# Macaron block (FFN, attention, FFN) on one core: the filler products of TensorE in the lead removed

## The reference

```python
x = x + 0.5 * ffn(layernorm(x))      # D = 128, H = 512, exact GELU
x = x + attn(layernorm(x))           # 16 heads of 64
x = x + 0.5 * ffn(layernorm(x))      # the same weights

# ffn: m1, m2 are outer products of 16 of the batch's own tokens
h   = gelu(x @ W1.T + scale * (x @ m1.T) + b1)
out = h @ W2.T + scale * (h @ m2.T) + b2
# attn: q, k with RMS norm per head; softplus gate on k; causal
bias   = -max(i - j, 0) * softplus(omega) * slope * gate[j]
scores = q @ k.T / 8 + bias
y      = softmax(scores) @ v ;  return y @ Wproj
```

## Time and profile before

| | |
|---|---|
| median of 3 runs | 755.38 us |
| the profiled execution | 754.96 us |
| its span, first to last instruction | 753.2 us |
| TensorE matmul busy | 729.2 us, 97% |
| VectorE, ScalarE, GpSimd busy | 655.4, 643.3, 645.4 us (87, 85, 86%) |

### The profile page before, as it was taken

One profiled execution on the slowest core, in us unless ns is written; L12 is line 12 of the kernel. 1 busy time (PEld: TensorE's weight loads), 2 busy tenths in 40 slices (PEclk: granted clock), 3 DMA queues, 4 the chain that ended last, 5 costly groups with the idle time before them and its releaser, 6 DMA issues.

```text
span 753.2 us, 25090 instructions
## 1 busy us (share of the span) xinstructions
PE 729.2 (97%) x9279; PEld 523.1 (69%) x9279; DVE 655.4 (87%) x2128; ACT 643.3 (85%) x1428; POOL 645.4 (86%) x760
## 2 busy tenths in 40 slices
PE   6789999999999999999999999999999999999997
PEld 4347667677768766787667777577776776677775
DVE  7889789988888798987989879888889879899986
ACT  8878798888988799888998889987998879986764
POOL 6738889898998999989998999989899898996791
DMA  6233315251345406333253423454043431435231
GB/s 176 41 93 80 73 36 138 58 113 33 73 99 100 101 3 125 77 87 87 44 104 63 102 64 72 87 102 103 14 104 84 100 87 26 105 73 113 61 58 29
DMA packets 98561, 60.05 MB, mean 80 GB/s; under 512 B 73566, under 2 KB 85344, under 8 KB 98440
## 3 DMA queue, kind: packets, MB, share of 16 engines
q1 hardware_dynamic: 98280, 57.93, 35.3%
q10 hardware_dynamic: 160, 0.52, 0.3%
HBM read 4.74 MB, written 2.10 MB: 9 GB/s over the span
## 4 chain that ended last, share of the span: by engine, by line
PE 63%; ACT 17%; DVE 12%; issue 5%; POOL 3%; DMA 0%; POOLq 0%; ACTq 0%; DVEq 0%
PE ps L1147 11%; PE ps L1149 10%; PE ps L1148 10%; PE ps L1294 8%; PE ps L1320 7%; PE ps L1321 7%; PE ps L1276 4%; ACT qk L1077 4%; DVE masked L1720 3%; PE ps L1322 3%; DVE ss L1684 2%; ACT pt L1102 2%; ACT qkn L1016 2%; ACT sq L1015 2%; ACT hid L1003 2%
## 5 line engine op out<-in xcount | busy, mean ns | idle before, releaser
L859 POOL TENSOR_TENSOR pt_l<-pt 128x512 f16<-128x512 f32 x366 | 320.2, 904 | 38.5 <-ACT pt L1102 38.2
L1720 DVE CUSTOM_DVE_ANT_0 masked<-ps,causal_row 128x512 f16<-128x512 f32 x480 | 205.8, 486 | 27.5 <-PE ps L1294 26.5
L1102 ACT ACTIVATE pt<-ps 128x512 f32<-128x512 f32 (+1 forms) x384 | 175.1, 534 | 16.6 <-PE ps L1322 16.4
L1320 PE MATMUL ps<-qk 128*128 128x512 f16 (+3 forms) x512 | 146.6, 299 | 0.1
L1321 PE MATMUL ps<-qk 128*128 128x512 f16 (+3 forms) x512 | 146.5, 299 | 0.0
L885 POOL TENSOR_TENSOR qkn<-qkn,rs 128x512 f32<-128x512 f32 x128 | 131.0, 1052 | 13.4 <-ACT rs L1027 12.8
L1147 PE MATMUL ps<-v_buf,pt 128*128 128x65 f16 x1280 | 129.7, 193 | 1.4 <-POOL pt_l L859 0.5
L1148 PE MATMUL ps<-v_buf,pt 128*128 128x65 f16 x1280 | 129.7, 193 | 0.0
L1149 PE MATMUL ps<-v_buf,pt_l 128*128 128x65 f16 x1280 | 129.5, 193 | 0.0
L1147 PEld LDWEIGHTS ps<-v_buf,pt 128*128 128x128 bf16 x1280 | 118.0, 98 | 6.7 <-issue 3.4
L1148 PEld LDWEIGHTS ps<-v_buf,pt 128*128 128x128 bf16 x1280 | 117.5, 98 | 1.8
(11 more groups left out here) (225 smaller groups left out, 1943.4 us busy)
## 6 DMA issues: line engine op xcount, KB each, us to landing
qk<-qk SPq DMA_DIRECT2D x128, 128.0 KB, 2.4
qk<-qk SPq DMA_DIRECT2D x62, 256.0 KB, 3.7
x_in<-in_L_attn_x SPq DMA_DIRECT2D x8, 256.0 KB, 3.1
out<-x_out SPq DMA_DIRECT2D x7, 256.0 KB, 2.3
qk<-qk SPq DMA_DIRECT2D x1, 1024.0 KB, 7.4
qk<-gtt SPq DMA_DIRECT2D x64, 8.0 KB
qk<-nmt SPq DMA_DIRECT2D x64, 2.0 KB
y_hl<-ytt SPq DMA_TRANSPOSE x62, 3.1
```

What stands on the lines that cost most here:

```text
L859: g.tensor_tensor(pt_l[:, h % 2, c], pt[:, h % 2, c], pt_h[:, h % 2, c], ALU.subtract).then_inc(s_pt_l, 1)
L1102: a.activation(pt[:, h % 2, c], ps[:, j, 0:width], ACT.Exp).then_inc(s_exp, 1)
L1320: pe.matmul(dst, k1(h)[:, keys], q1(h)[:, kb * P:T], start=True, stop=False)
L1720: ins = d.tensor_tensor_reduce(masked[:, part.unit(s, i)[0], col:col + (ib + 1) * P], part.bank(s, i)[:, col:col + (ib + 1) * P], causal_r ...
```

## The change

The seven `warm` entries of TensorE's lead go out of the table, with 6, 4, 5, 3, 6, 2 and 5 products, 31 in all. Each product goes with its weight load. The entry of `final` with 8 products, `keep_clock` itself, and the order of all other stages on all engines stay as they were. No wait is added or removed.

```diff
         "lead": [
-            ("setup", NEXT), ("zt", "a", NEXT), ("m", "a", NEXT), ("warm", 0, 6, NEXT), ("h", "a", NEXT),
-            ("out", "a", NEXT), ("warm", 1, 4, NEXT), ("uu", NEXT), ("warm", 1, 5, NEXT), ("zt", "att", NEXT),
-            ("warm", 1, 3, NEXT), ("qk", 0, 0, NEXT), ("qk", 0, 1, NEXT), ("qk", 0, 2, NEXT), ("qk", 0, 3, NEXT),
-            ("v", 0, 0, NEXT), ("qk", 1, 0, NEXT), ("v", 0, 1, NEXT), ("qk", 1, 1, NEXT), ("warm", 1, 6, NEXT),
-            ("qk", 1, 2, NEXT), ("qk", 1, 3, NEXT), ("t", 0, NEXT), ("gl", 0, NEXT), ("warm", 1, 2, NEXT),
-            ("t", 1, NEXT), ("qk", 2, 0, NEXT), ("qk", 2, 1, NEXT), ("warm", 1, 5, NEXT), ("gr", 0, NEXT),
+            ("setup", NEXT), ("zt", "a", NEXT), ("m", "a", NEXT), ("h", "a", NEXT),
+            ("out", "a", NEXT), ("uu", NEXT), ("zt", "att", NEXT),
+            ("qk", 0, 0, NEXT), ("qk", 0, 1, NEXT), ("qk", 0, 2, NEXT), ("qk", 0, 3, NEXT),
+            ("v", 0, 0, NEXT), ("qk", 1, 0, NEXT), ("v", 0, 1, NEXT), ("qk", 1, 1, NEXT),
+            ("qk", 1, 2, NEXT), ("qk", 1, 3, NEXT), ("t", 0, NEXT), ("gl", 0, NEXT),
+            ("t", 1, NEXT), ("qk", 2, 0, NEXT), ("qk", 2, 1, NEXT), ("gr", 0, NEXT),
```

## The result

The changed kernel took 759.42 us (median of 4, 758.63 to 761.3) against 755.36 for the kernel before (4, 754.7 to 755.49). The ratio is 1.0054 with a 95% interval of 1.0042 to 1.0066: it is slower by 4.1 us. The prediction had slower as the likeliest sign, but 757.0, and the measured median lies just above the end of its range, 759.4.

A forecast was written before the change was run, and what follows sets the result against it. TensorE, busy for 97% of the span, was taken to bound the kernel, with waits only in the lead. +2.1 - 0.09 - 0.43 = +1.6 us gave 756.6 on the profiled execution, 757.0 on the median; range 754.8 to 759.4.

The forecast's parts named there:

- Block 1: Six fillers before the hidden layer: without them its products start at the low clock level, +2.1 us.
- level high anyway: Rival: the level rises without the first six fillers and holds over the idle time; 754.9 us, chance 0.12.
- bounds of 1.1 and 2.35: Delay in us at the output product's end, for an early or a late rise of the level after 11.93 us.
- early count: Level rises 3.0 us after f16 products begin, f32 transposes not counting; whole change then about +0.6 us.
- count of slow products varies from run to run: Rule on spread: the changed kernel's runs would lie up to 1.25 us apart; the middle stays.
- Blocks 2 and 3: Fillers after the output product and before the transposes: removal frees only 0.09 us, since ScalarE is busy until 22.35.
- Blocks 4, 5 and 7: Fillers ahead of the first projection, at 29.34 and at 39.33 us: TensorE waits behind them anyway, so removal gives nothing.
- Block 6: Two fillers at 36.73 us, ahead of the second pair's transposes, on the path: removal frees 0.43 us.
- One for one to the end: Time the lead gains or loses reaches the kernel's end unchanged, as TensorE has no slack later.
- row of 199.14 us busy of 200: TensorE's busy time from 300 to 500 us, taken as evidence that no later batch takes up the delay.
- the prediction's own signs: Wrong if hidden products stand 0.22 us apart from the start, or the shift at 41 us differs from the end's.
- rival of a second drop: Level falls again later in the lead, at projections or between 33 and 43 us: +2.1, 759.1 us, chance 0.22.

The follow-up runs named there:

- h_after: The changed kernel with plain copies of y in place of the transposing DMAs; 758.31 us against 755.54 for the kernel before, ratio 1.0036.
- h_blocks234: Changed kernel with plain copies of y, the 4 + 5 + 3 fillers around the spread of u and the transposes put back; 756.17 us, ratio 1.0002.
- h_early_x: Changed kernel with plain copies of y, the load of batch 1's x moved forward in SyncE's queue; 757.56 us, ratio 1.0028.
- k_narrow31: Changed kernel with plain copies of y, plus 31 products of 8 columns ahead of the row of the gate, restoring TensorE's instruction count; 757.57 us, ratio 1.0024.
- k_delay11: Kernel before with plain copies of y, all fillers kept and 11 more added in the third filler block; 758.06 us, ratio 1.0041.
- m_b14_narrow13: Kernel before with plain copies of y, last three filler blocks out, 13 products of 8 columns where the last was; 755.09 us, ratio 0.9992.
- k_no_block6: Kernel before with plain copies of y, only the 2 fillers ahead of the second pair's transposes taken out; 755.84 us, ratio 1.0008.
- k_blocks1to4: Kernel before with plain copies of y, the last three filler blocks (6 + 2 + 5) taken out; 754.16 us, ratio 0.9987.
- m_converse97: Kernel before with plain copies of y, all fillers kept, 97 products of 8 columns added where TensorE waits; 756.11 us against 755.83, ratio 1.0004.

## Why the prediction was wrong, step by step

**Block 1, +2.1.** Right that the hidden layer would be slow and the delay on the path, too large for the profiled execution: 1.3 us (1.49 less the 0.21 of the first x) at the sum. The level had risen ahead of the gap, three products were fast and nine slow. That is half of the rival "level high anyway": it did rise behind the transposes, and then did not hold over the gap. In the traces of the other versions without block 1 the term is 1.2 (h_after) and 2.0 to 2.4 us (h_blocks234, h_early_x, k_narrow31, less the late first x): my bounds of 1.1 and 2.35 were right. The early count that I took from the Trainium skill ("TensorE: Matmul & The Clock Gate", Part 4) does not fit: in the changed kernel the level was up by 9.45 us (in k_delay11 by 8.9) after 2.6 us of f32 transposes and about 1 us (0.6 us) of f16 products. That the count of slow products varies from run to run (Part 1 of that page) holds: 9 of the 12 hidden products in the changed kernel, 8 in h_after, all 12 in h_blocks234, h_early_x and k_narrow31.

**Blocks 2 and 3, -0.09.** The visible part was right, 0.15 in the trace (1.49 to 1.33 at the low part of z). The step failed in what it left to a rival. Without these 9 products, and the 3 of block 4, the level fell at 23.1 us in the changed kernel, behind the spread of u (1.95 us on 16 rows of the array) and half of the transposes. The rival priced it at 0.6 to 2.5 for the first projections; it measured 1.4 (1.33 to 2.72), and putting blocks 2 to 4 back removed it. It came in every trace without them (five of five), so it was the likeliest case and not one of 0.22.

**Blocks 4, 5 and 7, nothing.** As gaps on the path, right: the earlier trace rows has 0.57 and 0.80 where the changed kernel has 1.29 and 1.87. But they do not guard the level surely either: it fell between 36 and 45 us in three of nine traces without blocks 5 to 7 (h_after, h_blocks234, m_b14_narrow13), and in two of five with 5 and 7 (k_delay11, k_no_block6).

**Block 6, -0.43.** Right: 0.40 (2.71 to 2.32), ScalarE's wait 1.07 to 0.67, again in k_blocks1to4.

**One for one to the end.** This step failed. For a delay it holds (k_delay11, k_narrow31). But the change also took 62 instructions out of TensorE's stream, and the fetches of that stream are DMA packets of their own. One moved from 61.0 us into the load of the next x, which landed in 4.95 us in place of 3.1; the statistics of batch 1 had no slack on it (68.68 in before, the load having landed at 68.65). That is 1.8 us, of which 1.1 stayed, and 0.7 to 0.9 more at 336 us came in both traces of the unfilled kernel and not in k_narrow31. The late transfer there is y: 4.3 and 4.5 us from issue to landing, with a fetch 1.2 and 1.6 us after the issue, against 2.4 in k_narrow31, whose fetch began as the copy was issued.

The copies of y show that this is no coincidence of three loads. In the twelve traces with plain copies, 459 of them have no fetch from 1.5 us before to 2.25 us after their issue, and took 2.2 to 2.9 us. With a fetch that began 0.5 to 1.5 us after the issue, 92 of them took 3.1 to 4.7 us, and the two groups do not overlap. My row of 199.14 us busy of 200 spoke of TensorE, and said nothing of the loads that its work waits for.

By the prediction's own signs two of its steps were wrong: the first hidden products stood 0.22 us apart, and the shift at 41 us, 2.3, is not that at the end, 4.4. The rival of a second drop, 759.1, comes near the median of 759.42 by luck. It puts 1.6 + 2.1 = 3.7 us in the lead, where the profiled execution has 2.3, and nothing behind it.

The sum as measured in the profiled execution: 0.2 (first x) + 1.3 + 1.4 - 0.15 - 0.4 = 2.3 in the lead, +1.1 at the load, +1.0 later, 4.4. As predicted: 2.1 - 0.5 = 1.6.

## What to carry to other kernels

A filler must be judged by what stands behind the next gap: here the 6 ahead of the hidden layer were worth 1.2 to 2.4 us of the lead and the 12 around the spread of u 1.2 to 1.8. Without the 13 behind them the median was 1.3 and 1.6 us lower, of which the traces show 0.4. Price every gap as a fall of the level first, and ask whether the work behind it is on the path. And count the instructions that an edit takes out or adds: where a load lands just as it is needed, a shifted fetch can cost as much as the fillers themselves (1.8 us at the first load here), and such a load is best issued earlier.

## What was not expected of the hardware

- A fetch of 16 KB of TensorE's instructions that began 0.2 to 0.3 us ahead of the first packets of the load of x, 256 KB in 512 packets, went with a time to landing of 4.3, 4.8 and 4.95 us (three of three, the 4.3 among other transfers), against 2.9 to 3.1 in the eleven other traces. One that began 0.7 us ahead of the load's packets did nothing (m_converse97). For the copies of y, also 256 KB, it was 3.1 to 4.7 us against 2.2 to 2.9.
- The kernel before is not at the high level throughout in every execution either. Of its 29 runs beside the h group, 17 had a mean granted clock of 1.000 and took 754.32 to 755.58 us; the 12 below that took 755.6 to 757.16. Beside the k and m groups the two kinds overlap, with medians 1.0 and 0.8 us apart.
- The granted clock of a trace has no entry for the low level ahead of its first recorded rise: it reads 1.00 while products stand 0.426 us apart (h_blocks234 from 12.24 us, recorded rise at 17.2). The trace of the kernel before has no entry at all.
